# Keys and values of six blocks made by rows from the two parts of x, the queries' order changed, and w1 and w2 staged in SBUF

## The reference

```python
Q, K, V = x @ wq.T, x @ wk.T, x @ wv.T             # 4096 x 64 each
energy  = K.T @ V                                  # 64 x 64, a sum over all tokens
out     = (Q @ energy) * sqrt(3 / 64) @ wo.T       # 4096 x 256
x = layernorm(x + out)
h = silu(x @ w1.T * s1) * (x @ w2.T * s2)          # 4096 x 1024
h = gelu(h @ h1.T * t1)
h = gelu(h @ h2.T * t2)
x = layernorm(x + h @ w3.T * s3)
```

## Time and profile before

| | |
|---|---|
| median of three runs | 647.01 us |
| the profiled execution, its own time | 647.28 us |
| its span, first to last instruction | 645.5 us |
| mean granted clock of TensorE | 0.999 |
| busy: TensorE, its weight loads | 635.5 us (98%), 531.1 us (82%) |
| busy: VectorE, ScalarE, GpSimd | 491.1 (76%), 411.0 (64%), 280.6 us (43%) |
| TensorE's share of the chain that ended last | 97% |

### The profile page before, as it was taken

The page is one execution under the profiler, slowest core; times in us unless marked ns, Lnnn a source line. Parts: engine busy times, 40 slices in busy tenths (PEclk is TensorE's granted clock), DMA queues, the critical chain, the costliest instruction groups (busy, mean ns, idle before and its releaser), DMA issues.

```text
span 645.5 us, 9171 instructions
## 1 busy us (share of the span) xinstructions
PE 635.5 (98%) x3147; PEld 531.1 (82%) x3148; DVE 491.1 (76%) x722; ACT 411.0 (64%) x697; POOL 280.6 (43%) x225
## 2 busy tenths in 40 slices
PE   8989999999999999999999999999999999999996
PEld 6768887888789888888889888888889888888896
DVE  5687799989565996789665898698754899488477
ACT  6579688868672566558661757656763466666655
POOL 0376999492001762096000564078000367069025
PEclk9999999999999999999999999999999999999999
DMA  8999889953310056434330036734330015534301
GB/s 342 391 367 401 321 333 354 378 205 130 133 67 0 2 163 229 162 131 147 129 116 1 1 97 191 251 118 159 130 131 1 0 20 188 184 131 144 118 1 67
DMA packets 24370, 103.89 MB, mean 161 GB/s; under 512 B 2224, under 2 KB 3312, under 8 KB 16496
## 3 DMA queue, kind: packets, MB, share of 16 engines
q1 hardware_dynamic: 24032, 102.98, 45.1%
q10 hardware_dynamic: 288, 0.26, 0.1%
HBM read 87.51 MB, written 23.07 MB: 171 GB/s over the span
## 4 chain that ended last, share of the span: by engine, by line
PE 97%; DVE 1%; issue 0%; POOL 0%; POOLq 0%; ACT 0%; DVEq 0%
PE ps L1395 63%; PE ps L1338 18%; PE ps L1464 8%; PE ps L1487 1%; PE ps L1270 1%; PE ps L1204 1%; PE ps L1232 1%; PE ps L1258 1%; PE ps L1246 1%; PE ps L1220 1%; PE ps L1252 0%; PE ps L1239 0%; DVE st L1125 0%; DVE xr L1132 0%; POOL rstd L512 0%
## 5 line engine op out<-in xcount | busy, mean ns | idle before, releaser
L1395 PE MATMUL ps<-R,ring 128*128 128x512 f32 x1792 | 410.2, 390 | 0.2 <-issue 0.2
L1395 PEld LDWEIGHTS ps<-R,ring 128*128 128x128 f32 x1792 | 335.2, 188 | 69.9 <-issue 0.6
L984 DVE TENSOR_TENSOR R<-quarter,R 128x512 fp32r<-128x512 f32 x284 | 262.0, 946 | 58.8 <-ACT R L709 58.5
L709 ACT CAST R<-quarter 128x512 fp32r<-128x512 f32 x284 | 173.2, 616 | 30.0 <-POOL quarter L540 12.0
L1338 PE MATMUL ps<-x1T,w 128*128 128x512 f32 x512 | 119.1, 391 | 0.6 <-issue 0.5
L755 ACT ACTIVATE quarter<-U,sc 128x512 f32<-128x512 f32 x96 | 69.5, 724 | 73.7 <-DVE U L1011 28.3
L1338 PEld LDWEIGHTS ps<-x1T,w 128*128 128x128 f32 x512 | 95.4, 188 | 21.9 <-ACT quarter L755 0.9
L530 POOL TENSOR_TENSOR quarter<-quarter,quarter 128x512 f32<-128x512 f32 x32 | 50.4, 1576 | 95.0 <-ACT quarter L755 88.3
L673 ACT ACTIVATE sg<-ps,sc 128x512 f32<-128x512 f32 x64 | 44.2, 690 | 63.6 <-PE ps L1338 63.5
L481 POOL TENSOR_TENSOR ve<-mv,eps 128x4 f32<-128x4 f32 x14 | 5.6, 403 | 180.4 <-DVE mv L961 180.4
L725 ACT COPY U<-ps 128x512 f32<-128x512 f32 x96 | 56.2, 585 | 28.7 <-PE ps L1395 28.5
(11 more groups left out here) (97 smaller groups left out, 389.1 us busy)
## 6 DMA issues: line engine op xcount, KB each, us to landing
ring<-combos SPq DMA_DIRECT2D x56, 1024.0 KB, 4.9
combos<-unit SPq DMA_DIRECT2D x8, 1024.0 KB, 8.5
unit<-in_h1T SPq DMA_DIRECT2D x4, 1024.0 KB, 14.6
xr<-in_x_rows SPq DMA_DIRECT2D x8, 512.0 KB, 5.1
unit<-in_h2T SPq DMA_DIRECT2D x4, 1024.0 KB, 8.7
xT<-in_xT SPq DMA_DIRECT2D x7, 512.0 KB, 7.7
out<-xr SPq DMA_DIRECT2D x7, 512.0 KB, 3.0
w<-w_dram SPq DMA_DIRECT2D x3, 1024.0 KB, 9.3
```

The source lines that it names most:

```text
L709: nc.scalar.copy(R[slot_of(p, u)][:, 0, c, :], quarter[operand_home(p, u)][:, c, :]).then_inc(hi_done, 1)
L984: nc.vector.tensor_tensor(r[:, 1, c, :], quarter[operand_home(p, u)][:, c, :], r[:, 0, c, :].bitcast(f32), ALU.subtract).then_inc(lo_done, 1)
L1395: last = nc.tensor.matmul(ps[:, bank + j, :], w, view(R[slot_of(p, u)][:, part, k, :]), start=n in (0, 1, 5) and k == 0 and part == 0, sto ...
```

## The change

Six things are edited:
- Keys and values of blocks 2 to 7 are made by rows, by `kv_of_parts`: 16 one-pass matmuls of 128 columns for each block, with the parts of x as weights. `kv_transposed`, the copies to `kvT` and `kv_turned` are gone. VectorE copies blocks 0 to 2 to `kv` (four buffers), ScalarE blocks 3 to 7.
- Pieces 0 to 11 of the queries stand ahead of the context and 12 to 31 behind it; `keep_clock(WARM_MIDDLE, 7)` is gone. `xhi` has eight buffers (four of them where `ring` lies) and no longer waits for the queries.
- The low part of x of block 1 is made by GpSimd, ahead of `combine(0)`.
- ScalarE's order: bits of unit 0 earlier, those of `w1` ahead of `T1s`, those of unit 1 behind `hi_of_transposed(0, 6)`, those of the sums of unit 0 ahead of those of unit 2.
- `w1` and `w2` are loaded to a stage in SBUF (where `U` lies) and from there to `w12`; their bits are read in the stage.
- SP's order: unit 0 ahead of the stages, the stores of the queries ahead of unit 4, units 3 and 4 behind waits for the stage.

GpSimd's order is otherwise as before, and so are `first_l1`'s `side` and VectorE's place for `normalise(0, 1, 1)`. Hunks that only declare names are left out, and context lines are cut.

```diff
@@ -32,7 +32,7 @@
-BIT_ORDER = [("wkv", 0), ("wq", 0), ("whole", 0), ("w12", 0), ("w12", 1), ("whole", 1), ("whole", 2), ("sums", 0), ("whole", 3),
+BIT_ORDER = [("wkv", 0), ("wq", 0), ("whole", 0), ("w12", 0), ("w12", 1), ("whole", 1), ("sums", 0), ("whole", 2), ("whole", 3),
@@ -49,13 +49,11 @@
-Q_BETWEEN = 4
+KV_DVE = 3
 FLAGS = 7
-Q_BANK = (4, 5, 6, 7, 5, 4, 5, 3)
+Q_BANK = (4, 5, 6, 7, 4, 6, 7, 4)
...
-
-WARM_MIDDLE = 5
@@ -143,7 +142,7 @@
-kv = [over(f"kv{i}", q_at + 2048 * i, [P, BLK]) for i in range(2)]
+kv = [over(f"kv{i}", q_at + (0, 2048, 9216, 11264)[i], [P, BLK]) for i in range(4)]
@@ -152,10 +151,11 @@
 wkvr = over("wkvr", q_at + 2 * 8192 + 2048, [P, EC, 2 * D], f32r)
-kvT = [over(f"kvT{i}", q_at + 8192 + 1024 + 2048 * i, [P, BLK]) for i in range(2)]
...
-xhi = [over(f"xhi{i}", x1T_at + 4096 * i, [P, EC, BLK], f32r) for i in range(4)]
+xhi = [over(f"xhi{f}", x1T_at + 4096 * f if f < 4 else ring_at + 4096 * (f - 4), [P, EC, BLK], f32r) for f in range(NB)]
+
+w12_stage = over("w12_stage", u_at, [P, 2 * EC * HID])
@@ -230,7 +230,7 @@
-    return (1, 3, 2)[f] if f < 3 else f + 1
+    return 1 if f == 0 else f
@@ -310,14 +310,14 @@
-    def relay_w12(i):
+    def stage_w12(i):
         at = i * EC * HID
-        sp.dma_start(w12_dram[:, at:at + EC * HID], (w1_in, w2_in)[i]).then_inc(w12_relayed[i], 16)
+        sp.dma_start(w12_stage[:, at:at + EC * HID], (w1_in, w2_in)[i]).then_inc(w12_staged[i], 16)
...
         at = i * EC * HID
-        sp.wait_ge(w12_relayed[i], 16)
-        sp.dma_start(w12[:, at:at + EC * HID].bitcast(f32), w12_dram[:, at:at + EC * HID]).then_inc(w12_in[i], 16)
+        sp.wait_ge(w12_staged[i], 16)
+        sp.dma_start(w12[:, at:at + EC * HID].bitcast(f32), w12_stage[:, at:at + EC * HID]).then_inc(w12_in[i], 16)
@@ -327,6 +327,9 @@
             sp.wait_ge(l1_tile, 2 * HC * (i - 5))
+        if 3 <= i <= 4:
+            sp.wait_ge(w12_in[i - 3], 16)
+            sp.wait_ge(bits_done, n_bits("w12", i - 3))
@@ -360,9 +363,9 @@
         sp.dma_start(dst, src).then_inc(cst_in, 16)
-    relay_w12(0)
-    relay_w12(1)
     load_unit(0)
+    stage_w12(0)
+    stage_w12(1)
@@ -371,16 +374,16 @@
     store_unit(0)
+    relay_hidden(0, 0)
     store_q(4)
-    relay_hidden(0, 0)
-    load_unit(4)
-    store_unit(1)
...
     store_q(7)
-    store_unit(2)
+    load_unit(4)
+    store_unit(1)
...
     relay_hidden(0, 1)
+    store_unit(2)
@@ -551,6 +554,10 @@
+    pool.wait_ge(kv_ready, 2)
+    pool.wait_ge(xhi_done, 2)
+    nc.gpsimd.tensor_tensor(tiles_of(xlo[1]), tiles_of(xT[1]), xhi[1].bitcast(f32).rearrange("p c (t n) -> p c t n", t=TPB),
+                            ALU.subtract).then_inc(second_xlo, 1)
@@ -596,10 +603,12 @@
-    def copy_kvt(f):
-
-        act.wait_ge(kvt_ready, f - 1)
-        nc.scalar.copy(kvT[f % 2][:, :], ps[:, KV_BANK[f], :]).then_inc(kvt_out, 1)
+    def copy_kv(f):
+
+        act.wait_ge(kv_ready, f + 1)
+        if f >= 4:
+            act.wait_ge(et_ready, f - 3)
+        nc.scalar.copy(kv[f % 4][:, :], ps[:, KV_BANK[f], :]).then_inc(later_kv_out, 1)
@@ -608,13 +617,11 @@
             act.wait_ge(x_first, 16)
-        if f >= 4:
-            act.wait_ge(q_ready, f - 3)
-        nc.scalar.copy(xhi[f % 4].rearrange("p c (t n) -> p c t n", t=TPB), tiles_of(xT[f])).then_inc(xhi_done, 1)
+        nc.scalar.copy(xhi[f].rearrange("p c (t n) -> p c t n", t=TPB), tiles_of(xT[f])).then_inc(xhi_done, 1)
     def bits_of_w12(i):
-        act.wait_ge(w12_in[i], 16)
-        bits(low_halves(w12[:, i * EC * HID:(i + 1) * EC * HID]), 0, i)
+        act.wait_ge(w12_staged[i], 16)
+        bits(low_halves(w12_stage[:, i * EC * HID:(i + 1) * EC * HID]), 0, i)
@@ -826,44 +833,42 @@
         high_x(f)
-    copy_kvt(2)
...
     high_x(5)
-    copy_kvt(3)
+    high_x(6)
+    copy_kv(3)
+    high_x(7)
+    copy_kv(4)
     hi_of_q(1)
-    high_x(6)
-    copy_kvt(4)
+    copy_kv(5)
+    bits_of_whole(0)
+    copy_kv(6)
     raw_q(2)
-    high_x(7)
-    raw_q(3)
-    for f in range(5, NB):
-        copy_kvt(f)
-    bits_of_whole(0)
-    raw_q(4)
+    copy_kv(7)
+    bits_of_w12(0)
...
     nc.scalar.activation(T1s[:, 0, :], ps[:, 3, 0:E], ACT.Copy, scale=CTX_SCALE).then_inc(t1_hi, 1)
-    for i in range(2):
-        bits_of_w12(i)
-    bits_of_whole(1)
+    bits_of_w12(1)
+    raw_q(3)
+    raw_q(4)
...
     raw_q(6)
+    raw_q(7)
     hi_of_transposed(0, 6)
-    raw_q(7)
+    bits_of_whole(1)
...
         silu(0, j, A)
-        if j == 0:
-            bits_of_whole(2)
+        if j <= 1:
+            bits_of_sums(0, range(j, j + 1))
         if 2 <= j <= 3:
-            bits_of_sums(0, range(j - 2, j - 1))
+            bits_of_whole(j)
...
             hi(0, 0, j - KH)
-        if j == 5:
-            bits_of_whole(3)
@@ -911,10 +916,10 @@
     def low_x(f):
-        if f < 2:
-            dve.wait_ge(kv_ready, f + 1)
+        if f == 0:
+            dve.wait_ge(kv_ready, 1)
         dve.wait_ge(xhi_done, f + 1)
-        nc.vector.tensor_tensor(tiles_of(xlo[f]), tiles_of(xT[f]), xhi[f % 4].bitcast(f32).rearrange("p c (t n) -> p c t n", t=TPB),
+        nc.vector.tensor_tensor(tiles_of(xlo[f]), tiles_of(xT[f]), xhi[f].bitcast(f32).rearrange("p c (t n) -> p c t n", t=TPB),
@@ -1091,24 +1096,23 @@
     nc.vector.memset(zeros[:, :], 0.0).then_inc(zeros_made, 1)
-    for f in range(NB):
+    def copy_kv(f):
         dve.wait_ge(kv_ready, f + 1)
-        if f >= 2:
-            dve.wait_ge(et_ready, f - 1)
-        nc.vector.tensor_copy(kv[f % 2][:, :], ps[:, KV_BANK[f], :]).then_inc(kv_out, 1)
-        if f == 0:
-            low_x(0)
-            flag_out(0)
-        elif f == 1:
-            low_x(2)
-            low_x(1)
-            low_x(3)
-            low_x(4)
-            lo_of_q(0)
-        elif f <= 4:
-            if f == 4:
-                lo_of_q(1)
-            low_x(f + 3)
+        nc.vector.tensor_copy(kv[f][:, :], ps[:, KV_BANK[f], :]).then_inc(kv_out, 1)
+
+    copy_kv(0)
+    low_x(0)
+    flag_out(0)
+    copy_kv(1)
+    low_x(2)
+    low_x(3)
+    low_x(4)
+    copy_kv(2)
+    lo_of_q(0)
+    low_x(5)
+    low_x(6)
+    low_x(7)
+    lo_of_q(1)
@@ -1197,10 +1201,10 @@
                 if b >= 4:
-                    pe.wait_ge(*((qlo_done, 2), (qlo_done, 1), (q_raw, 3), (tile_sum[0], TPB))[b - 4])
+                    pe.wait_ge(*((qlo_done, 1), (q_raw, 1), (q_raw, 2), (q_raw, 3))[b - 4])
             if part == 1 and c == 0:
-                pe.wait_ge(xlo_done, n_xlo(b))
-            x = xhi[b % 4][:, c, :] if part == 0 else tiles_of(xlo[b])[:, c, :, :]
+                pe.wait_ge(*((second_xlo, 1) if b == 1 else (xlo_done, n_xlo(b))))
+            x = xhi[b][:, c, :] if part == 0 else tiles_of(xlo[b])[:, c, :, :]
@@ -1221,28 +1225,27 @@
-    def kv_transposed(f, view):
-
-        if f > 2:
-            pe.wait_ge(kv_out, f - 2)
-        for part in range(2):
-            pe.wait_ge(*((xhi_done, f + 1) if part == 0 else (xlo_done, n_xlo(f))))
-            for c in range(EC):
-                x = xhi[f % 4][:, c, :] if part == 0 else tiles_of(xlo[f])[:, c, :, :]
-                last = nc.tensor.matmul(ps[:, KV_BANK[f], :], wkvr[:, c, :] if view is exact else wkv[:, c, :], view(x),
-                                        start=part == 0 and c == 0, stop=part == 1 and c == 1)
-        last.then_inc(kvt_ready, 1)
-
-    def kv_turned(f):
-        pe.wait_ge(kvt_out, f - 1)
+    def kv_of_parts(f, view):
+
+        if f >= 3:
+            pe.wait_ge(*kv_copied(f - 3))
+        pe.wait_ge(xhi_done, f + 1)
+        pe.wait_ge(xlo_done, n_xlo(f))
         for q in range(TPB):
-            last = nc.tensor.transpose(ps[:, KV_BANK[f], q * P:(q + 1) * P], kvT[f % 2][:, q * P:(q + 1) * P], ident[:, :])
+            for part in range(2):
+                for c in range(EC):
+                    x = xhi[f][:, c, q * P:(q + 1) * P] if part == 0 else tiles_of(xlo[f])[:, c, q, :]
+                    last = nc.tensor.matmul(ps[:, KV_BANK[f], q * P:(q + 1) * P], view(x), wkvr[:, c, :] if view is exact else wkv[:, c, :],
+                                            start=part == 0 and c == 0, stop=part == 1 and c == 1)
...
+    def kv_copied(f):
+        return (kv_out, f + 1) if f < KV_DVE else (later_kv_out, f - KV_DVE + 1)
...
     def energy(f):
-        pe.wait_ge(kv_out, f + 1)
+        pe.wait_ge(*kv_copied(f))
         for q in range(TPB):
-            k, v = kv[f % 2][:, q * P:q * P + D], kv[f % 2][:, q * P + D:(q + 1) * P]
+            k, v = kv[f % 4][:, q * P:q * P + D], kv[f % 4][:, q * P + D:(q + 1) * P]
@@ -1321,8 +1324,6 @@
             pe.wait_ge(gelu_done, n_gelu(2 * p - 1, 1, t))
-        elif t == 3:
-            pe.wait_ge(q_raw, NB - 2)
@@ -1514,36 +1515,33 @@
         q_pieces(range(4), view)
-        for f in range(2, NB):
-            kv_transposed(f, view)
-            if f <= Q_BETWEEN:
-                q_pieces(range(4 * (f - 1), 4 * f), view)
-            if f == 2:
-                energy(1)
-            else:
-                kv_turned(f - 1)
-            if f >= 4:
```

(37 more changed lines are left out.)

## The result

| | before | after |
|---|---|---|
| median of the runs | 647.05 us (646.89 to 647.16) | 655.86 us |
| profiled execution, its own time | 647.28 us | 652.11 us |
| its span, mean granted clock | 645.5 us, 0.999 | 650.2 us, 0.999 |

The changed kernel is slower: ratio 1.0127, 95% interval 1.0086 to 1.0168. Its executions differ far more than those of before: 652.11 (clock 0.999), 655.71 (0.992), 656.01 (0.994), 657.16 (0.991), and one of 668.78 (0.971) that the ratio leaves out. I had forecast 651.1 us. The profiled execution is close to that and the median is not, so there are two questions: where 4.7 us of span went in the profile, and what the others have besides.

The account below looks back on a forecast made before the run. TensorE, 98% busy, was taken as the bound. TensorE up to the last energy +1.9, normalisation of block 0 -1.0 and the late combination +3.2 made +4.1 us on 647.01: 651.1 us, range 645.0 to 654.0 us.

Parts of the forecast that it names:

- the late combination: GpSimd's combination of unit 1 ends later, so TensorE waits for `normalise` at the transposes of block 1: +3.2 us, bounds 0 and 4.
- the one on the clock: TensorE's new 3.2 us wait would not lower the granted clock, judged from the end of the earlier profile: nothing added.
- TensorE up to the last energy: TensorE's work from first queries to last energy, with 96 narrow matmuls at 0.123 us: 19.9 us against 17.96, +1.9 us.
- The rivals with 0.076 and with 0.255 us: Price per 128-column matmul of keys and values: 0.076 gives 646.6 us, chance 0.27; 0.255 gives 663.8 us, chance 0.10.
- What feeds it: Low parts of x from VectorE and GpSimd reach TensorE's front about in time: 0, bounds 0 and +1 us.
- Normalisation of block 0: Without GpSimd's combination beside it, VectorE's last tile takes 0.35 us and ends earlier: -1.0 us, bounds 0 and -1.0.
- The sum without the clock: Whole kernel: +1.9 - 1.0 + 3.2 = +4.1 us on 647.01, giving 651.1 us, nothing added for the clock.
- Queries behind the context: Six more pieces, 1.4 us, fit the stretch between last energy and dense first layer, with `keep_clock` gone: 0.
- copies: Copies to `kvT` go and five to `kv` move to ScalarE, covered by energies 5 and 6: 0, up to 0.5 uncovered.
- stage in SBUF: w1 and w2 move the same bytes in two steps and are wanted only near the dense first layer: 0.
- SP's order: Unit 3 waits on SP for the bits of w1; the store of unit 0 behind it is not ready earlier: 0.

Follow-up runs that it names:

- the repeated run: The changed kernel run again with no edit, against the kernel before: median 654.01 us, ratio 1.0097.
- the execution of 660.35 us: Changed kernel with GpSimd's inverse deviation of block 1 ahead of unit 2, wait on `norm_done` kept; one of three executions at 660.2 to 660.5 us, median 649.44.

## Why the prediction was wrong

The direction and the largest new wait, that for the late combination, were right: the profiled execution has +4.8 us (652.11 against 647.28), forecast were +4.1. Measured was a median of +8.8, outside the range.

- **The step that failed is the one on the clock**: "A wait of 3.2 us is inside what it outlasted there, so I add nothing." The tail of the kernel before is one reading of one stretch without work. Behind a wait of 2.9 us the clock fell in the profile of the repeated run for 3.4 us; behind two waits of about 1.4 us for at least 6 us; behind one of 1.5 us in the kernel before without its zeros; behind waits of 0.5 and 0.8 us for some 27 us in the execution of 660.35 us. It happens in some executions and not in others, and the profile of the result was one where it had not: the term put at nothing is the 3.6 to 5.1 us that the other executions near the median have over it. The changed kernel has three such waits. With all three filled or removed, eleven of twelve executions came within 1.5 us of each other, and again eleven of twelve within 1.6 us with the buffer in DRAM; the twelfth took 655.04 and 663.11 us.
- **TensorE up to the last energy**, +1.9 forecast, +1.42 measured, and that nearness is luck. The 1.42 us are 0.09 us of a later start (10.38 against 10.29 us), the 0.93 us of waiting of the next point, and only 0.4 us of more work where 1.9 were forecast. The price of a narrow matmul was 0.11 us (1.74 us for 16), forecast 0.123, which is 1.2 us for the 96: it is near the 0.11 us that was read for the load of its weights, and the 0.016 us on top that the 256-column row has are hardly there. The rivals with 0.076 and with 0.255 us fall. The Trainium skill's 81 ns ("TensorE: Matmul & The Clock Gate", section "Back-to-back issue gap") is not met by these float32 operands; its 107 ns for the load (section "LDWEIGHTS") is within 5% of what was measured.
- **What feeds it**, forecast 0 within 0 to +1: it cost 0.93 us, counted in the 1.42. The low part of block 2 started at 9.97 us, 0.5 us behind GpSimd's subtraction, and took 2.97 us; the next two took about 1.2 us each, with GpSimd idle. So VectorE did not crawl, as the prediction has it, but did nearly all of its work after GpSimd's instruction had ended at 11.86 us. The row it took the crawl from was misread: the three tiles did not take 0.73 us each. Two took 0.39, and the last, the only one beside GpSimd's combination, took the 1.36 us that the earlier trace rows shows. Held until 11.86 us and then 1.16 us gives 13.0 us, where the text has 12.1.
- **Normalisation of block 0**, forecast -1.0: the three tiles took 1.25 us, as said. But behind the last energy nothing was won (+0.28), since TensorE began the transposes 1.8 us after the flag (36.73 to 38.56 us), where it had been 1.1. The forecast took the last tile for what the transposes wait for, and had no term for this second path. This is the wait called "issue" at the branch that takes the flag. What makes it 1.0 us in one kernel and 1.9 in another stays open.
- **The combination of unit 1, late**, forecast +3.2: measured 2.93, by the path that was written down, and confirmed by two ways of taking it away.
- **The sum without the clock**, +4.1 forecast and +4.8 in the profiled execution, is near because errors cancel: 1.4 us too much for TensorE's work and 0.3 for the late combination, against 0.9 too little for the feeding and 1.3 too little for block 0.
- **Queries behind the context, copies, stage in SBUF, SP's order**, forecast 0: right. `keep_clock` in the same breath, "with `keep_clock` gone", was not: its work costs nothing, but its absence does.

What stays open is which of the three waits made the low stretches of the four other executions of the result, of which there is no profile, and why a stretch is once 3 us long and once 27. The repeated run and the experiments show all three places at work.

## What to carry to other kernels

Count a new wait of the bounding engine twice: its own length, and a stretch at half the clock that follows it in some executions and costs half its length (3.4 to 27 us long here); dummy work laid into a wait is there for the second, and makes it rarer, not impossible. A forecast from one profile of a kernel with new waits is a forecast of its best executions, so look at the spread and the mean clock before believing a median. When a helper's step is moved behind another one, follow its whole queue to the next thing that somebody else needs: here four combinations, a deviation and a normalisation hung on one reading of bits.

## What the hardware showed that I had not expected

- VectorE is held for the length of a GpSimd instruction, not slowed by a share. Its tensor_scalar between SBUF and SBUF took 0.35 us alone (1.38 for four) and 1.35 us beside GpSimd's instructions of 1.26 to 1.29 us (5.40 for four), ending about 0.15 us after each. Its subtraction with all operands in SBUF took 1.16 to 1.21 us alone and 2.97 beside GpSimd's of 2.38 us, ending 1.1 us after it. A mean over instructions of which only some overlap hides this: 5.23 us for three, or 2.19 for three tiles.
- A one-pass float32 matmul with weights of its own starts 0.111 us after the last one at 128 columns, 0.123 at 256 and 0.229 at 512. At a granted clock of 0.50 the narrow ones start 0.21 us apart (two in 0.43 us, in the profile with the filled wait):

```profile
16.07 0.63 PE L1238 MATMUL ps<-wkvr,xhi 128*128 128x128 f32 x2
16.49 0.63 PE L1238 MATMUL ps<-wkvr,xlo 128*128 128x128 f32 x2
```

A load of 128 columns takes 0.33 us there (mean of 17 at 16 to 20 us) and 0.19 at the full clock. So the load, which is what I take to bound them, follows the granted clock too.
